# An LSTM followed by a GRU on one core: the LSTM's input products from step 24 on as seven block products for two steps

## The reference, cut to what matters

```python
# LSTM, per step t                      # GRU, per step t; vz, vr, vh are constant over t
a = x_t @ Wx + b + h @ Wh               z = sigmoid(y_t @ W_z + g @ U_z + vz)
i, f, o = sigmoid(a[:, :3*512])...      r = sigmoid(y_t @ W_r + g @ U_r + vr)
g_ = tanh(a[:, 3*512:])                 c = tanh(y_t @ W + (r * g) @ U + vh)
c = f * c + i * g_                      g = (1 - z) * g + z * c
h = o * tanh(c);  y_t = x_t + h         out_t = y_t + g
```

## Time and profile before

| | us |
|---|---|
| median of 3 runs (lowest to highest) | 1232.53 (1230.04 to 1233.65) |
| the profiled execution's own time | 1231.82 |
| its span, first to last instruction | 1229.9 |
| PE busy / DVE busy / ACT busy / POOL busy | 1200.8 / 872.1 / 445.0 / 277.8 |
| mean granted TensorE clock | 0.992 of full speed |

### The profile page before, as it was taken

How to read it: one execution, slowest core, us unless ns; L and a number is a source line. 1 busy time by engine, 2 the same in 40 slices (tenths; PEclk the granted TensorE clock), 3 DMA queues, 4 the chain that set the end, 5 groups by cost and what they waited for, 6 DMA issues and landing times.

```text
span 1229.9 us, 68313 instructions
## 1 busy us (share of the span) xinstructions
PE 1200.8 (98%) x31174; PEld 823.2 (67%) x31174; DVE 872.1 (71%) x2681; ACT 445.0 (36%) x1078; POOL 277.8 (23%) x520
## 2 busy tenths in 40 slices
PE   5889999999999999999999999999999999999998
PEld 1457676676666766766666667667666676676665
DVE  2668877777777777777777777777777777777765
ACT  5555233333333333333333333333333333333332
POOL 3100222222222222222222221222222222222221
PEclk9899999999999999999999999999999999999999
DMA  9900100111110111110011110011111001110001
GB/s 309 323 7 10 21 17 8 21 21 21 21 21 6 18 21 20 21 21 11 13 21 21 21 21 17 8 21 21 21 21 21 10 14 21 21 21 12 12 4 29
DMA packets 142066, 39.51 MB, mean 32 GB/s; under 512 B 135825, under 2 KB 136081, under 8 KB 140753
## 3 DMA queue, kind: packets, MB, share of 16 engines
q1 hardware_dynamic: 140080, 34.49, 12.4%
q0 software_dynamic: 640, 0.53, 0.2%
q10 hardware_dynamic: 1056, 0.13, 0.1%
HBM read 26.74 MB, written 8.39 MB: 29 GB/s over the span
## 4 chain that ended last, share of the span: by engine, by line
PE 93%; SPq 3%; DVE 2%; DMA 1%; issue 0%; ACT 0%; DVEq 0%
PE ps_l L797 52%; PE ps_g L797 38%; PE ps_g L806 3%; SPq L241 2%; DMA o_area<-in_L_cond_C_dram 1%; SPq L245 1%; PE ps_l L806 1%; DVE zr L552 0%; DVE wh L549 0%; DVE u L549 0%; SPq L250 0%; ACT zr L468 0%; SPq L252 0%; DVE rgT L732 0%; PE ps_c L806 0%
## 5 line engine op out<-in xcount | busy, mean ns | idle before, releaser
L797 PE MATMUL ps_l<-wh,h2T 128*32 128x512 f16 x5952 | 345.6, 380 | 3.3 <-DVE wh L549 3.3
L797 PE MATMUL ps_l<-wx,x2T 128*32 128x512 f16 x6020 | 348.5, 379 | 0.0
L797 PEld LDWEIGHTS ps_l<-wx,x2T 128*32 128x32 f16 x6020 | 179.5, 97 | 119.7
L797 PE MATMUL ps_g<-w,y2T 128*32 128x384 f16 x5760 | 256.4, 326 | 0.0
L797 PEld LDWEIGHTS ps_l<-wh,h2T 128*32 128x32 f16 x5952 | 171.3, 97 | 123.3 <-DVE wh L549 3.6
L797 PEld LDWEIGHTS ps_g<-w,y2T 128*32 128x32 f16 x5760 | 173.2, 97 | 73.4
L328 POOL TENSOR_TENSOR yT<-xT,hT 128x128 f32<-128x128 f32 x128 | 61.8, 483 | 581.6 <-DVE hT L681 581.6
L797 PE MATMUL ps_g<-u,g2T 128*32 128x256 f16 x5760 | 179.6, 273 | 1.0 <-ACT g2T L496 1.0
L797 PEld LDWEIGHTS ps_g<-u,g2T 128*32 128x32 f16 x5760 | 159.8, 97 | 11.5 <-issue 1.4
L552 DVE SCALAR_TENSOR_TENSOR zr<-ps_g,sc,term 128x256 f32<-128x256 f32 x128 | 61.9, 484 | 99.4 <-PE ps_g L797 92.8
L312 POOL TENSOR_TENSOR o_area<-yT,gT 128x128 f32<-128x128 f32 x127 | 58.2, 458 | 298.3 <-DVE gT L780 298.3
(11 more groups left out here) (103 smaller groups left out, 1108.7 us busy)
## 6 DMA issues: line engine op xcount, KB each, us to landing
x_nat<-in_x_dram SPq DMA_DIRECT2D x126, 64.0 KB, 2.6
out_dram<-o_area SPq DMA_DIRECT2D x124, 64.0 KB, 2.1
wh<-in_L_cond_Wx_dram SPq DMA_DIRECT2D x4, 1024.0 KB, 10.9
w<-in_L_cond_Wh_dram SPq DMA_DIRECT2D x3, 1024.0 KB, 18.7
u<-in_L_cond_Wh_dram SPq DMA_DIRECT2D x1, 1024.0 KB, 24.2
stage<-in_L_cond_W_z_dram SPq DMA_DIRECT2D x1, 1024.0 KB, 8.6
stage<-in_L_cond_W_r_dram SPq DMA_DIRECT2D x1, 1024.0 KB, 8.3
stage<-in_L_cond_W_dram SPq DMA_DIRECT2D x1, 1024.0 KB, 10.5
```

Of the source, the lines that this page charges most:

```text
L797: mm = nc.tensor.matmul(bank[B * j:B * j + B, c0:c1].rearrange("p (n c) -> p n c", c=B), still(a, k), moving(b, k, j), start=opens and (a, ...
```

## The change

From step FW = 24 on the LSTM's input products of the steps u (even) and v = u + 1 are computed together by seven block products in place of eight. A11, A12 are the two halves (over the contraction) of x_u, A21, A22 those of x_v; Bij are the four 256 x 1024 quarters of Wx. T1 to T4 are differences of such quarters, S1 to S4 sums and differences of the A blocks:

- T1 = B12 - B11, T3 = B22 - B12, T2 = B22 - T1, T4 = B21 - T2;
- S1 = A21 + A22, S3 = A11 - A21, S2 = S1 - A11, S4 = A12 - S2;
- the products are A11 B11, A12 B21, S1 T1, S2 T2, S3 T3, S4 B22 and A22 T4, each of 6 quads of moving width 256 (`seventh`).

Three and a half of them stand in the `wx` stage of each tick, 21 quads. At an even tick t = u: S3 T3 of this pair, then for the pair u + 2 the second half of A22 T4, A11 B11, and S1 T1 (into the bank `ps_fifth`). At an odd tick, for u = t + 1: S2 T2, A12 B21, S4 B22; and for u = t + 3 the first half of A22 T4.

Partial results that serve several outputs are read out of PSUM by DVE into `pre` (f32, 128 x 256 each, `evict`): `first_out` and `fifth_out` of pair u + 2 at even ticks (behind the candidate's sum, and behind g's transpose), `sixth_out` at odd ticks (behind the candidate's sum), and `seventh_out(t)` at even ticks, behind `keep`. `seventh_out(u)` empties the upper half of the bank of step v = u + 1, in which v's `wh` stage then accumulates; PE at an odd tick waits for it (`evicted`) before the `wh` stage. The gate sums add `pre` in place of the bias.

Beside that: at tick 9 Wx (4 MB) is loaded again; in ticks 11 to 14 POOL makes the T's (`make_t`, two differences of 128 x 1024 a tick); ACT makes their HI parts behind its work in ticks 12, 13, 15, 16 (128 x 2048 each), DVE their LO parts, two of 128 x 1024 a tick in ticks 13, 14, 16 and 17. POOL makes the S's of a group at q = 3 (four of 128 x 256), ACT splits them and x at q = 0, DVE at q = 1. DVE's group tasks have other places from group 5 or 6 on: `lstm_scales` at q = 0, LO of x at q = 1, `largest` at q = 2 and `turn_out` at q = 3 stand behind the gate sums; `turn` stands at q = 3 and LO of S at q = 1 behind `keep`. The stores go out two ticks before their old place, in the same order.

```diff
+        N2 = SLAB // 2
+        wx_again = [stage[:, k, :] for k in range(K)]
+        b11, b12 = stage[:, 0:2, 0:N2], stage[:, 0:2, N2:]
+        b21, b22 = stage[:, 2:4, 0:N2], stage[:, 2:4, N2:]
+        t1, t3, t4, t2 = b11, b12, b21, b22
+        N_T1, N_T3, N_T2, N_T4 = range(4)
+        def parts(slab):
+            return stage[:, slab, :].bitcast(f16).rearrange("p (a k n) -> p a k n", a=2, k=2)
+        t_parts = [parts(4), parts(5), parts(0), parts(1)]
+        t_whole = [t1, t3, t2, t4]
+        pre = stage[:, 2, :].rearrange("p (t n) -> p t n", t=NL)
+        xs = stage[:, 3, 0:Q * P]
+        xs2 = stage[:, 3, Q * P:3 * Q * P].bitcast(f16).rearrange("p (r a n) -> p r a n", r=2, a=2)
+        def blocks(x_group):
+            v = x_group.rearrange("p (m s h c) -> p m s h c", m=2, s=2, h=2)
+            return [v[:, :, a, b, :] for a in range(2) for b in range(2)]
+        def in_pairs(n):
+            return xs[:, P * n:P * n + P].rearrange("p (m c) -> p m c", m=2)
+        T_AGAIN, T_MADE = 9, 11
...
-                if t >= 2 * Q + 1 and t % Q == (1 if t < T else 0):
-                    store(Q * (group - 2), r, group - 2)
+                if t == T_AGAIN:
+                    sp.wait_ge(cand_ps, F - 1)
+                    sp.wait_ge(w1_split, HALVES * GG)
+                    sp.wait_ge(u1_split, HALVES * GG)
+                    for k in range(K):
+                        sp.dma_start(wx_again[k], wx[P * k:P * k + P, :]).then_inc(again_in, 16)
+                if q == Q - 1 and group >= 1:
+                    store(Q * (group - 1), 1 - r, group - 1)
...
+            def make_t(to, of, less):
+                for k in range(2):
+                    if pool_made[0] >= 2:
+                        pool.wait_ge(t_made, pool_made[0] - 1)
+                    nc.gpsimd.tensor_tensor(to[:, k, :], of[:, k, :], less[:, k, :], ALU.subtract).then_inc(t_made, 1)
...
+                s1, s2, s3, s4 = (in_pairs(m) for m in range(4))
+                before = 4 * (group - NG_W)
+                pool.wait_ge(xT_done, group + 1)
+                if group > NG_W:
+                    pool.wait_ge(xs_lo, group - NG_W)
+                else:
+                    pool.wait_ge(t_split, 4 * HALVES)
+                nc.gpsimd.tensor_tensor(s1, a21, a22, ALU.add).then_inc(xs_done, 1)
+                nc.gpsimd.tensor_tensor(s3, a11, a21, ALU.subtract).then_inc(xs_done, 1)
+                pool.wait_ge(xs_done, before + 1)
+                nc.gpsimd.tensor_tensor(s2, s1, a11, ALU.subtract).then_inc(xs_done, 1)
+                pool.wait_ge(xs_done, before + 3)
+                nc.gpsimd.tensor_tensor(s4, a12, s2, ALU.subtract).then_inc(xs_done, 1)
...
+                if t == T_MADE:
+                    pool.wait_ge(again_in, 16 * K)
+                    make_t(t1, b12, b11)
+                if t == T_MADE + 1:
+                    make_t(t3, b22, b12)
+                if t == T_MADE + 2:
+                    make_t(t2, b22, t1)
+                if t == T_MADE + 3:
+                    make_t(t4, b21, t2)
+                if q == Q - 1 and NG_W <= group + 2 < NG:
+                    make_s(r, group + 2)
...
+            def split_high(n):
+                act.wait_ge(t_made, 2 * n + 2)
+                hi_part(t_parts[n][:, HI], t_whole[n], col["a_wx"], t_hi)
...
+                if q == 0 and NG_W <= group + 1 < NG:
+                    act.wait_ge(xT_done, group + 2)
+                    act.wait_ge(scl_done, group + 2)
+                    nc.scalar.mul(x2T[:, 1 - r, HI, :], xT[:, 1 - r, :], a_x(1 - r)).then_inc(x_hi, 1)
+                    act.wait_ge(xs_done, 4 * (group + 2 - NG_W))
+                    nc.scalar.mul(xs2[:, 1 - r, HI, :], xs, a_x(1 - r)).then_inc(xs_hi, 1)
+                if T_MADE + 1 <= t <= T_MADE + 2:
+                    split_high(t - T_MADE - 1)
+                if t == T_MADE + 4:
+                    act.wait_ge(t_split, 2 * HALVES)
+                    split_high(N_T2)
+                if t == T_MADE + 5:
+                    split_high(N_T4)
...
+            def t_low(n, half):
+                dve.wait_ge(t_hi, n + 1)
+                lo_part(t_parts[n][:, LO, half], t_whole[n][:, half], col["a_wx"], t_parts[n][:, HI, half]).then_inc(t_split, 1)
...
+                if T_MADE + 2 <= t <= T_MADE + 3:
+                    t_low(t - T_MADE - 2, 0)
+                if T_MADE + 5 <= t <= T_MADE + 6:
+                    t_low(t - T_MADE - 3, 0)
...
+            H1, H2 = slice(0, 2 * P), slice(2 * P, 4 * P)
+            def bias0(half):
+                return term0[:].rearrange("p g c -> p (g c)")[:, half]
+            def evict(n, u, to, ps, term):
+                dve.wait_ge(seven_ps, 2 * (u - FW) + n)
+                undone(to, ps, r_l(u // Q % 2), term).then_inc(evicted, 1)
+            def first_out(u):
+                evict(1, u, pre[:, u % NL, H1], ps_l[(u + 1) % NL][:, H2], bias0(H1))
+            def fifth_out(u):
+                evict(2, u, pre[:, (u + 1) % NL, H2], ps_fifth[:, H1], bias0(H2))
+            def sixth_out(u):
+                dve.wait_ge(evicted, 2 * (u - FW) + 2)
+                evict(3, u, pre[:, u % NL, H2], ps_l[(u + 1) % NL][:, H2], pre[:, (u + 1) % NL, H2])
+            def seventh_out(u):
+                evict(4, u, pre[:, (u + 1) % NL, H1], ps_l[(u + 1) % NL][:, H2], bias0(H1))
...
+                        dve.wait_ge(evicted, 2 * (t - FW) + 3 if t % 2 == 0 else 2 * (t - FW) + 2)
+                    to_add = pre[:, t % NL, :] if t >= FW else term0[:].rearrange("p g c -> p (g c)")
+                    undone(gates[:, 3 * P:4 * P], ps_l[t % NL][:, 3 * P:4 * P], r_l(r), to_add[:, 3 * P:4 * P]).then_inc(tg_sum, 1)
+                    undone(ifo, ps_l[t % NL][:, 0:3 * P], r_l(r), to_add[:, 0:3 * P]).then_inc(ifo_sum, 1)
+                if q == 0 and NG_W <= group + 1 < NG:
+                    lstm_scales(1 - r, group + 1)
+                if q == 1 and NG_W <= group + 1 < NG:
+                    dve.wait_ge(x_hi, group + 1)
+                    lo_part(x2T[:, 1 - r, LO, :], xT[:, 1 - r, :], a_x(1 - r), x2T[:, 1 - r, HI, :]).then_inc(x_lo, 1)
+                if q == 2 and NG_W <= group + 2 < NG:
+                    dve.wait_ge(x_in[r], 16 * J * (i + 2))
+                    largest(r)
+                if q == 3 and group >= 1 and t < T:
+                    dve.wait_ge(out_done[1 - r], 16 * J * ((group - 1) // 2 + 1))
+                    turn_out(1 - r, group - 1)
...
+                if FW <= t < T and q % 2 == 0:
+                    seventh_out(t)
...
+                if q == 3 and NG_W <= group + 2 < NG:
+                    dve.wait_ge(yT_done, t + 1)
+                    turn(r)
+                if q == 1 and NG_W <= group + 1 < NG:
+                    dve.wait_ge(xs_hi, group + 2 - NG_W)
+                    lo_part(xs2[:, 1 - r, LO, :], xs, a_x(1 - r), xs2[:, 1 - r, HI, :]).then_inc(xs_lo, 1)
...
+                    if FW <= t + 2 < T and q % 2 == 0:
+                        first_out(t + 2)
+                    if FW <= t + 1 < T and q % 2 == 1:
+                        sixth_out(t + 1)
...
+                    if FW <= t + 2 < T and q % 2 == 0:
+                        fifth_out(t + 2)
...
+            FOURTH = 3
+            halves = [(a, b, k) for a, b in PASSES for k in range(K // 2)]
+            def seventh(bank, half, operand, weights, opens, first=0, last=len(halves)):
+                for a, b, k in halves[first:last]:
+                    for j in range(J):
+                        mm = nc.tensor.matmul(bank[rows(j), 2 * P * half:2 * P * half + 2 * P].rearrange("p (n c) -> p n c", c=B),
+                                              operand(a, k),
+                                              weights(b, k).rearrange("p (n j c) -> p j n c", j=J, c=B)[:, j],
+                                              start=opens and (a, b, k) == halves[0], stop=(a, b, k) == halves[-1],
+                                              skip_group_check=True)
+                return mm
...
+                    if t >= FW and q % 2 == 1:
+                        pe.wait_ge(evicted, 2 * (t - FW) + 2)
...
-                if FL - 1 <= t < T - 1:
+                if FL - 1 <= t < FW - 1:
                     if t == FL - 1:
                         pe.wait_ge(wx_split, K)
@@ -952,9 +1165,45 @@
                     if q == Q - 1:
                         pe.wait_ge(x_lo, group + 1)
                     product(ps_l[(t + 1) % NL], 0, GL * P, wx_of, x_of((n + 1) % U // Q, (n + 1) % Q), 0, END, True, False)
-                if q == 0 and 0 < group < NG - 1:
+                if q % 2 == 0:
+                    if FW <= t < T:
+                        pe.wait_ge(evicted, 2 * (t - FW) + 3)
+                        seventh(ps_l[(t + 1) % NL], 1, s_of(r, 3, q // 2), t_of(N_T3), False).then_inc(seven_ps, 1)
+                    if FW <= t + 2 < T:
+                        u, v = t + 2, t + 3
+                        ru, qu = u // Q % 2, u % Q
```

(45 more changed lines are left out.)

46 lines of the change are left out of this document (36 added, 10 removed).

## The result

The changed kernel takes 1251.76 us, median of 4 runs (1249.91 to 1252.6). The kernel before, on the same chip, takes 1231.28 (1229.93 to 1233.65). The ratio is 1.0155, with a 95% interval of 1.0139 to 1.0171: slower, by 20.5 us. The profiled execution took 1252.6 with a span of 1250.7; before it was 1229.9, so 20.8 us are to be placed.

The account below looks back on a forecast made before the run. PE was taken to bound the kernel (busy 98% of the span, 93% of the last chain). 1231.8 us + 9.5 (steady part and way in) + 8 (making the T's) = 1249, range 1237 to 1271.

Parts of the forecast that it names:

- four steady ticks: Sum of the changes of D over q = 0 to 3: +0.29 us per group, +7.5 over 26 groups.
- making the T's: Splits of the T's on DVE and ACT in ticks 12 to 17 cost 8 us, between 0 and 18.
- The matmuls: PE, per pair of steps: 42 quads at 0.109 us, 4.58, replace 24 at 0.216, 5.18; 0.60 less.
- Odd ticks: The GRU's chain sets D: 3.02 us at q = 3, 3.08 at q = 1; 0.24 and 0.18 less than before.
- D: PE's distance from the start of the wx stage to the start of the next wh stage; 3.26 us before.
- the 0.18: Cost in us of PE coming out of a wait, read from tick 127: 0.85 instead of 0.67 to the successor.
- Even ticks: PE's wh stage of the following odd tick waits for seventh_out behind keep: D = 3.63 us, bounds 3.55 and 3.75.
- The third rival: Even D near 3.45, making the T's hidden, time within 1229 to 1236 us; chance 0.04.
- The first rival: seventh_out does not set the pace; D is 3.02 or 3.08 in all ticks, time 1217 us; chance 0.12.
- the second rival: POOL's long instructions block DVE at z*c, g and LO of g and in ticks 11 to 14: 1270 us; chance 0.15.
- the reserve of about 1 us: DVE's idle time before zr, 0.39 to 1.04 us, taken to absorb most lateness from the moved group tasks.
- The way in from tick 21: Ticks 21 to 23, where old and new quads mix on PE: +0.33, +1.64 and -0.24, together +1.7 us.

Follow-up runs that it names:

- the first experiment: The changed kernel with seventh_out moved on DVE ahead of the LO part of h: 1227.01 us, ratio 0.9948 to the kernel before.
- narrow differences: The changed kernel with POOL's eight differences for the T's cut from 1024 to 64 columns (wrong output): 1237.83 us, ratio 1.004 to the kernel before.
- the third experiment: The changed kernel with the old 12-quad products throughout and no first_out to seventh_out, T's and S's made but unused: 1250.33 us, ratio 1.0133 to the kernel before.

## Why the prediction was right in its total and wrong in two of its terms

The forecast was 1249, the result 1251.8, and the mechanism on which it was put is there. But the total is close by luck: two errors of opposite sign, 8.5 and 9.4 us, nearly cancel. Counted on the same stretches:

| term | predicted | measured |
|---|---|---|
| four steady ticks | +0.29 | -0.18 |
| ticks 26 to 126 (25 groups) | +7.2 | -1.3 |
| making the T's, ticks 12 to 19 | +8 | +17.4 |
| ticks 21 to 26 | +1.9 | +2.3 |
| start, tail | 0 (+0.2) | +2.5 |

**The matmuls: right.** 21 quads take 2.29, the 0.109 per quad of the earlier trace rows.

**Odd ticks: too dear by 0.03 and 0.11.** I had D at 3.02 (q = 3) and 3.08 (q = 1), by the GRU's chain. Measured are 2.99 and 2.97, and that is PE's own time (2.29 + 0.67, at q = 3 `bound` besides). HI of r*g ends 2.23 after the stage's start, 0.06 before the stage is over (600.35 + 0.29 against 598.41 + 2.29). The 2.17 that I read from tick 127 was right for the chain; the 0.18 for coming out of a wait was not. It was the step of the working that failed in the steady part, and it was a misreading of the earlier trace rows.

**The 0.18.** I took the 0.85 from HI of r*g's end to the start of the next stage, 0.18 more than the usual 0.67, for the price of a wait. But behind tick 127 the next stage is not `wh`, as in all ticks before, but `w`, and `w` waits itself, for ACT's HI of y. Two rows of before, the first from the end, the second from the start of tick 10, before which `u c` waits as well:
```profile
1217.45 0.30 ACT L479 CAST y2T<-y_scaled 128x128 f16<-128x128 f32 x1 [1.41 <-POOL y_scaled L333]
```
```profile
142.45 2.78 PE L797 MATMUL ps_l<-wh,h2T 128*32 128x512 f16 x48
```
The cast ends at 1217.75 and `w` starts at 1217.89, 0.14 behind it, and this distance is 0.14 in all eight kernels here. In tick 9 `u c` starts at 141.78 out of a wait of 0.35, and `wh` follows 0.67 behind it, as without a wait. After, the five `u c` stages that wait in ticks 9 to 18 take 0.67 or 0.68 too. So coming out of a wait costs the 0.05 to 0.06 from the producer's end to the first matmul, and the chain's own bound at odd ticks was 2.17 + 0.05 + 0.67 = 2.89, less than PE's 2.96.

**Even ticks: the mechanism right, the size off by 0.17.** `seventh_out` starts 2.92 after the stage's start (I had 2.94) and takes 0.47 (0.48). Then I added 0.21 for coming out of two waits, and measured are 0.06: 592.49 to 592.55. The mis-sized term is this one, by the same misreading. After the wait the `wh` stage takes 2.60 like any other. Even D = 2.92 + 0.47 + 0.06 = 3.45, below my lower bound of 3.55, since all the bounds were varied about the same 0.13 to 0.18. Twice 0.17 and the odd ticks' 0.14 (0.03 and 0.11) make up 0.48, about the 0.47 between +0.29 and -0.18 per group.

**The third rival** (even D near 3.45, chance 0.04) had the even D exactly, but also that making the T's is hidden, which failed. **The first rival** is what the first experiment turns on: it said that S3 T3 is ready 1.6 us before DVE comes to it, which is 2.1 (its last matmul ends at 589.93); it named 2.84 as the end of the clearing that frees PE, and D of 3.0; with the clearing's end at 2.94 it measured 3.00, since PE gets going 0.06 behind it. Its 35.5 for four ticks became 35.36.

**Making the T's: the wrong cause, and 9.4 too little.** I priced it by tick 9 of before, where DVE's and ACT's split work made PE late, and set POOL at 1 us. That part alone, for which I had 7 of the 8, is 4.0 with narrow differences. The rest was the second rival's mechanism, to which I gave 0.15, with the low clock that goes with its longest wait (2.5), which I had nowhere. I had the rule that describes the mechanism: the Trainium skill, "SBUF — State Buffer", section "Who interferes with whom", says that DVE and GpSimd share a port pair that is an exclusive lock, and, of DVE's two-port modes, that the one that issues first holds it for its whole instruction and the other blocks fully. I let speak against it, with 0.09 us on `keep`. That row holds: POOL's `y_scaled` ran from 130.02 to 130.73 with `keep` (130.26, 0.37) inside it, so for this pair the trace does not agree with the rule, and the measurement decides. The steady ticks say the same: at 591.00 `y_scaled` runs for 0.64, and DVE's LO of r*g, with two operands from SBUF, stands inside it (591.29) for 0.35, as long as LO of g with no POOL instruction beside it (594.64). But `y_scaled` is a tensor_scalar with one large input. I carried it over to POOL's tensor_tensor, for which my only row had DVE first; there the two excluded one another. With a tensor_tensor on POOL first the traces agree with the rule: z*c, g, and `keep` in the first experiment all end 0.14 to 0.15 behind POOL's. The length was off as well: I had POOL's differences at up to 3.7 us, they take 2.4.

In steady ticks the second rival costs nothing, though the sign that I had named for it, z*c or g over 0.3 at q = 3, is there. There I had also written down the S differences wrongly: they are four instructions of 128 x 128 elements, not of 128 x 256, 0.46 to 0.51 each. At q = 3 they lengthen z*c and g, in the timeline after:
```profile
620.67 0.46 POOL L391 TENSOR_TENSOR stage<-xT 128x128 f32<-128x128 f32 x1
620.79 0.49 DVE L952 TENSOR_TENSOR zc<-zr,cand 128x128 f32<-128x128 f32 x1
...
621.32 0.43 DVE L955 TENSOR_TENSOR g_nat<-zc,keep 128x128 f32<-128x128 f32 x1
```
0.21 and 0.14 more than usual, and the reserve of about 1 us covers it: PE without idle time in the third experiment shows that.

**The way in from tick 21: near.** 2.3 against 1.9; ticks 21 to 23 took what I had, tick 24 took 0.86 more than before, where I had 0.34. **The start** (+2.3) lies before anything of the change has run: the `wh` of tick 5 starts at 92.17 instead of 89.88 already. PE's last wait for a transfer of the weights ends at 50.9 instead of 49.7, which is 1.2 of it. The other 1.1 come between there and 92 us, and there the granted clock is lower: 0.83 against 0.91 from 40 to 60 us, 0.92 against 0.99 from 80 to 100. The `wh` of tick 12 starts between 161.0 and 162.5 in the six other kernels. All of these are above the 160.67 of before, so a few tenths may belong to what they have in common with the change; that is not settled.

**What stays open.** Ticks 26 to 126 by their pattern would take 25 x 36.29 = 907.2; they take 910.3. The 3.1 us are in single ticks, at most 0.55 in one: most in ticks 43 to 48, 60, 72, 83, 95 and 125. In ticks 60 and 72 PE's weight loads pause with no releaser, such as this one after:
```profile
620.47 1.82 PEld L979 LDWEIGHTS ps_l<-wh,h2T 128*32 128x32 f16 x36 [0.61 <-issue]
```
The kernel before and the one of the third experiment (480 matmuls and weight loads a tick, with the seven products 552) show none in that stretch (at most 0.09 in one tick of the latter). That it goes with the number of instructions is a guess and was not tried.

## What to carry to other kernels

An instruction for which another engine waits belongs on an in-order queue at the place of its need: behind `keep` this one held back 26 x 0.93 = 24 of the 26 x 1.11 = 29 us that the steady ticks can gain, and moving it ahead of two instructions brought 24.7. Beside a chain on DVE whose instructions read two operands from SBUF, a long tensor_tensor on POOL cost that chain up to nearly its whole length (2.06 of 2.42 us), though it was itself not on the path; cut it into short pieces, or give the work to DVE in the gaps in which it waits. A stage that stands in for the one of interest must have the same successor: the last tick had another, and a term read from it was wrong by 0.13. And a total that agrees proves no term: compare stretch by stretch before believing the account.
